# An attention and mixture-of-experts block: down product behind the first up product, mask products a step later, weight loads behind the high half

## The chip, the cores and the metric

The kernel runs on one core of a Trainium2 chip. The metric is the device time of one execution in microseconds. TensorE multiplies, VectorE and ScalarE do the elementwise work, GpSimd subtracts and issues gathers, SyncE's queue issues most transfers. The engines run their own instruction lists in order and meet at semaphores.

## The reference, cut to what matters

The block is an adaptive layer norm with linear attention, then a second layer norm with a feed-forward part of eight routed experts (two per token) and one shared expert:

```python
h = _layernorm(x) * (1 + ca) + sa
x = x + ga * attn(h)                      # linear attention, 16 heads of 32
h = _layernorm(x) * (1 + cb) + sb
scores = sigmoid(h @ gate_w.T)
idx = top_k(scores + router_bias, 2); w = scores[idx] / sum(scores[idx])
out = sum over the two experts of w * (silu(h @ W1[e]) * (h @ W3[e])) @ W2[e]
shared = (silu(h @ sw1.T) * (h @ sw3.T)) @ sw2.T
x = x + gb * (out + shared)
```

There are 4096 tokens of width 512; an expert has an inner width of 352, the shared expert of 704.

## The kernel before

All matrices are kept as a high and a low half in float16, and a product is three matmuls (high by high, high by low, low by high; lines 84 to 86). Tokens are worked in 32 tiles of 128.

The kernel has four stages. First the attention, a loop of slots `s`, in which tile s is projected and tile s - 8 is finished. From slot 32 on, only the finishing is left (the tail, slots 32 to 42), and the shared expert starts beside it. Then the shared expert goes on alone while the router picks experts and makes the token list. Then the routed experts run over 71 slot tiles. At the end the shared expert's last seven chunks run beside the combining of the results.

The shared expert works in chunks of two tiles, and a chunk in six steps, one for each 128 columns of the inner width (the sixth is 64 wide). Steps are numbered through: q = 6n + j. Each step has one piece on each engine:

- TensorE, `up(q)`: 24 products (12 in a sixth step) into one of three PSUM banks. It waits for `multiply(q - 3)`, which frees the bank.
- ScalarE, `activate(q)`: the silu from PSUM into `s_act`, of which there are two buffers; it waits for `up(q)` and for `low(q - 2)`. Then `high(q - 1)`, the cast of the previous step's product into the high half of `s_at`. With j = 0 it waits for the previous chunk's down product, since `s_at` has one buffer for each j.
- VectorE, `multiply(q)`, then `low(q - 1)`, the low half of `s_at`.
- Once per chunk TensorE's `down(n - 1)` multiplies the six pieces of `s_at` of the finished chunk by `sw2`: for each of its two tiles 17 products, in the order of j, each j of the first tile waiting for its low half. VectorE's `add(n - 1)` then joins it to the residual `s_xs`, and SyncE stores it and loads the next.

`down_due(q)` says at which steps down and add are issued: at j = 1 in the tail (q below 22), at j = 2 after it. Chunk 9's step 54 is left out; its down product runs among the experts.

Beside the steps run other things, in a table `beside` on VectorE: the selection of the experts (steps 22 to 24), the counts (`add_runs` and `place`, steps 25 and 26). In step 24 TensorE forms the ranks from `both`. From step 27 to step 42 VectorE makes the masks of two tiles in each step (`masks`: `lane_is` and two `tile_is` for each tile, lines 870 and 873; four buffers, freed by the products), between `multiply(q)` and `low(q - 1)`, and TensorE multiplies them in the same step (line 1381). In step 43 (`LIST_STEP`) `list_tokens` reads the sum and gives `slot_token`, on which the experts' gathers and the last 22 weight pieces wait (they lie where the names of the router lie).

The experts' weights, 88 pieces, are loaded into a ring of four staging buffers (`w_stage`) by loads issued on ScalarE's queue (`w_loads`, line 1056), each after the piece four before it has been converted. ScalarE casts each (line 1075). For pieces 22 to 65 it also rescales it in place (line 1078), and GpSimd subtracts (line 468); for the others VectorE makes the low half (line 688). `w_turn(q)` spreads the pieces over the steps: 44 over the steps up to `LIST_STEP`, the last 22 over the steps from there to step 50.

The orders of the engines in steps 22 to 53 are written out by hand:

Of the kernel before, what the change touches and what calls it, by code (L numbers as in the profile page):

```python
# [17 lines left out]
TILES = T // P  # L18
# [5 lines left out]
SH_TILES = 6  # L24
# [18 lines left out]
TAIL_STEPS = STEPS_PER_SLOT * TAIL  # L43
CHUNKS = TILES // 2
EARLY = 9
EARLY_STEPS = SH_TILES * EARLY
X_RING, QT_RING, HT_RING, XR_RING, X2_RING, H2T_RING, STAGE_RING, W_RING, Y_RING, YB = 4, 9, 3, 2, 3, 3, 6, 4, 4, 8
# [7 lines left out]
LISTED = 3  # L55
PICKED = 4
BIG = 1e30
LIST_STEP = TURNS_FROM + TILES // TURNS_PER_STEP
LAST_PIECES = 3
SHARED_PIECES = (E - 2) * WP  # L60
GB_LOADS = 16 * (4 + B)
# [57 lines left out]


def down_due(q):
    return q >= SH_TILES and q % SH_TILES == (1 if q < TAIL_STEPS else 2) and q // SH_TILES != EARLY


def list_turn(q):
    first = TURNS_PER_STEP * (q - TURNS_FROM)
    return range(first, first + TURNS_PER_STEP) if 0 <= first < TILES else range(0)
# [22 lines left out]
def sync_program(nc, m, sp):  # L150
# [196 lines left out]
    for q in range(EARLY_STEPS, SH_TILES * CHUNKS):  # L347
        n, j = q // SH_TILES, q % SH_TILES
        if j == 1:
            load_h(n + 1)  # L350
        if down_due(q):
            store_xs(n - 1)
            load_xs(n)
        r = early_turn(q)
        if r is not None:
            store_out(r)
            load_xc(r + Y_RING)
# [154 lines left out]
def vector_program(nc, m, v):  # L512
# [194 lines left out]
    for s in range(-3, TILES + TAIL):  # L707
# [34 lines left out]
        if s >= TILES:  # L742
            q = STEPS_PER_SLOT * (s - TILES)
            multiply(q)
            low(q - 1)
            if down_due(q):
                add(q // SH_TILES - 1)
        h2_low(t - 2)
        v_low(s)
# [26 lines left out]
        if s >= TILES:  # L776
            q = STEPS_PER_SLOT * (s - TILES)
            for p in w_turn(q):
                w_low(p)
            multiply(q + 1)  # L780
            low(q)
            if down_due(q + 1):
                add((q + 1) // SH_TILES - 1)
            for p in w_turn(q + 1):
                w_low(p)
# [110 lines left out]
    for q in range(TAIL_STEPS, EARLY_STEPS):  # L896
        multiply(q)
        for t in list_turn(q):
            masks(t)
        low(q - 1)  # L900
        if q > LIST_STEP:
            for p in w_turn(q):
                w_low(p)
        for work in beside.get(q, ()):
            work()
        if down_due(q):
            add(q // SH_TILES - 1)
    low(EARLY_STEPS - 1)

# [29 lines left out]
    for q in range(EARLY_STEPS, SH_TILES * CHUNKS):  # L939
        n, j = q // SH_TILES, q % SH_TILES  # L940
        multiply(q)
        if q > EARLY_STEPS:
            low(q - 1)
        if down_due(q):
            add(n - 1)
        t = early_turn(q)
        if t is not None:
            combine(t)
# [4 lines left out]
def scalar_program(nc, m, act):  # L953
# [88 lines left out]
    def high(q):  # L1042
        if q < 0:
            return
        n, j = q // SH_TILES, q % SH_TILES
        w = step_width(j)
        act.wait_ge(m.act_done, q + 1)
        if j == 0:
            at_least(act, m.sy_done, 2 * n)
        act.activation(m.s_at[0:w, j, 0, :], m.s_act[0:w, q % 2, :], ACT.Copy).then_inc(m.at_hi, 1)  # L1050
# [9 lines left out]
    def w_loads(last):  # L1060
        nonlocal w_next
        while w_next <= last:
            w_load(w_next)
            w_next += 1
# [24 lines left out]
    for s in range(-3, TILES + TAIL):  # L1089
# [48 lines left out]
                w_load(p)  # L1138
        if s >= TILES:
            q = STEPS_PER_SLOT * (s - TILES)  # L1140
            w_loads(q + W_RING - 1)
            activate(q)
            high(q - 1)
            h2_high(t - 2)
            convert_weights(q)
            w_loads(q + W_RING)
            activate(q + 1)
            high(q)
            convert_weights(q + 1)
# [8 lines left out]
    act.wait_ge(m.logits_ready, 1)  # L1158
    act.activation(m.scores[:, :, :], m.logits[:, :, 0:E], ACT.Sigmoid).then_inc(m.scores_ready, 1)
    for q in range(TAIL_STEPS, EARLY_STEPS):  # L1160
        if w_turn(q):
            w_loads(w_turn(q)[0] + W_RING - 1)
        activate(q)
        high(q - 1)
        convert_weights(q)
    high(EARLY_STEPS - 1)

# [34 lines left out]
def tensor_program(nc, m, pe):  # L1202
# [164 lines left out]

    for q in range(TAIL_STEPS, EARLY_STEPS):
        up(q)
        if q == TAIL_STEPS + 2:  # L1370
            pe.wait_ge(m.both_ready, 1)
            pe.wait_ge(m.r_consts, 5)
            for part, lhs in ((0, m.before), (1, m.ones)):
                nc.tensor.matmul(m.ps_r[:, part, :], lhs[:, :], m.both[:, :, :].rearrange("p t e -> p (t e)"),
                                 start=True, stop=True).then_inc(m.ranks_done, 1)
        if down_due(q):
            down(q // SH_TILES - 1)
        for t in list_turn(q):
            for k in range(TOP):
                pe.wait_ge(m.pair_ready, (1 + TOP) * t + 2 + k)  # L1380
                nc.tensor.matmul(m.ps_list.rearrange("p t n -> p (t n)"), m.lane_is[:, t % PAIR_RING, k, :],  # L1381
                                 m.tile_is[:, t % PAIR_RING, k, :, :].rearrange("p t n -> p (t n)"),
                                 start=t == 0 and k == 0, stop=t == TILES - 1 and k == TOP - 1, skip_group_check=True).then_inc(m.pair_used, 1)
# [343 lines left out]
```

## Time and profile before

| | us |
|---|---|
| median of three runs | 1451.88 |
| lowest and highest run | 1448.08, 1453.30 |
| profiled execution | 1449.57 |
| its span | 1447.8 |
| busy in the span: TensorE products | 1264.5 |
| VectorE | 666.1 |
| ScalarE | 435.1 |
| GpSimd | 438.4 |
| mean granted clock of TensorE | 0.942 |

Busy times are those of the profile; ends of matmuls are modelled, so TensorE's share is an upper value. The profile also divides the span into 40 slices of 36 us, and gives each wait the operation that ended it. A number behind a time in brackets is idle time of the engine ahead of the row.

In the time of the span the stages lie as follows: the tail of attention from 436 to about 577 us, the shared expert with router and token list from there to 828, the routed experts from 838 to 1268, the last stage from there to the end.

### The profile page before, as it was taken

Reading aid. Unit: us, or ns where it says so; the run is one execution under the profiler, and the core shown is the slowest. Engines: PE = TensorE matmul, PEld = TensorE weight load, DVE = VectorE, ACT = ScalarE, POOL = GpSimd, SP = SyncE. Lnnn points to the kernel's source line nnn. Section 1 sums busy time; section 2 is a strip of 40 time slices with the busy share of each in tenths; the row PEclk is TensorE's granted clock in tenths of the full one; section 3 lists DMA queues with packets and bytes.
Section 4 is the critical chain, followed back from the end, with each engine's and each line's share of the span. In section 5 each row is a group of like instructions: output and inputs, shape, how many; then the busy total and the mean of one; then the engine's idle time right before and its main releaser. Section 6 shows DMA issues by size and latency. Waiting matters only on the chain.

```text
span 1447.8 us, 25298 instructions
## 1 busy us (share of the span) xinstructions
PE 1264.5 (87%) x9054; PEld 795.8 (55%) x9054; DVE 666.1 (46%) x1338; ACT 435.1 (30%) x913; POOL 438.4 (30%) x411
## 2 busy tenths in 40 slices
PE   6898998998997789556658789999999999989998
PEld 2545655665665557333325446566656665566664
DVE  4555867777776646653444521111111111125455
ACT  2433434443433324422232412222222222211211
POOL 1213655655553322321121011111111111146542
PEclk9999999999998989867778889999999999999999
DMA  5714787888968557222121555655555556569886
GB/s 183 223 48 123 186 182 186 215 188 185 209 174 239 168 144 217 63 89 67 50 76 44 162 129 132 133 134 132 132 131 138 140 134 133 114 191 243 227 216 171
DMA packets 269205, 219.09 MB, mean 151 GB/s; under 512 B 188496, under 2 KB 200784, under 8 KB 268572
## 3 DMA queue, kind: packets, MB, share of 16 engines
q1 hardware_dynamic: 241560, 158.45, 42.9%
q0 software_dynamic: 12848, 35.40, 10.7%
q10 hardware_dynamic: 14680, 23.62, 5.4%
q8 instruction: 80, 1.31, 0.4%
q14 instruction: 37, 0.30, 0.1%
HBM read 116.69 MB, written 56.94 MB: 120 GB/s over the span
## 4 chain that ended last, share of the span: by engine, by line
PE 53%; DVE 12%; DMA 10%; POOL 10%; issue 9%; ACT 4%; SPq 1%; ACTq 0%; DVEq 0%; POOLq 0%
PE ps_o L84 6%; PE ps_o L85 6%; PE ps_o L86 6%; PE ps_vs L84 5%; PE ps_vs L86 5%; PE ps_vs L85 5%; DMA xt<-g 2%; DVE tile_is L873 2%; DMA yb<-y_d,slot 2%; DMA wp_raw<-in_wproj_t 2%; PE ps_kh L84 2%; PE ps_vh L84 2%; PE ps_vh L85 2%; PE ps_vh L86 2%; PE ps_kh L86 2%
## 5 line engine op out<-in xcount | busy, mean ns | idle before, releaser
L84 PE MATMUL ps_o<-w_all,xt 128*128 x568 | 178.7, 315 | 15.6 <-DMA xt<-g 15.2
L477 POOL DMA_INDIRECT g<-h_d,slot_token x71 | 67.9, 956 | 391.2 <-DMA xt<-g 348.7
L85 PE MATMUL ps_o<-w_all,xt 128*128 x568 | 178.7, 315 | 0.0
L86 PE MATMUL ps_o<-w_all,xt 128*128 x568 | 178.6, 314 | 0.0
L920 DVE TENSOR_TENSOR at<-ps_y,at 128x384 f16<-128x384 f32 x71 | 39.6, 558 | 176.6 <-ACT at L1176 176.6
L1181 ACT ACTIVATE y<-ps_vs,slot_weight 128x512 f32<-128x512 f32 x71 | 48.8, 688 | 230.6 <-PE ps_vs L86 230.6
L915 DVE SCALAR_TENSOR_TENSOR a<-ps_o,a 128x352 f32<-128x352 f32 x71 | 37.3, 525 | 173.3 <-PE ps_o L86 173.3
L468 POOL TENSOR_TENSOR w_all<-w_stage,w_all 128x352 f16<-128x352 f32 (+2 forms) x44 | 45.0, 1033 | 166.5 <-ACT w_stage L1078 166.1
L84 PE MATMUL ps_qh<-ht,wqkv 128*128 128x128 f16 x512 | 87.5, 219 | 7.3 <-DVE qt L555 4.9
L656 DVE TENSOR_TENSOR s_at<-s_act,s_at 128x256 f16<-128x256 f32 x80 | 35.3, 441 | 125.1 <-ACT s_at L1050 115.4
L84 PE MATMUL ps_kh<-s_ht,sh 128*128 128x256 f16 x256 | 78.1, 305 | 16.8 <-DVE s_act L644 9.6
L86 PE MATMUL ps_qh<-ht,wqkv 128*128 128x128 f16 x512 | 87.4, 219 | 0.0
L85 PE MATMUL ps_qh<-ht,wqkv 128*128 128x128 f16 x512 | 87.4, 219 | 0.0
L1381 PE MATMUL ps_o<-tile_is,lane_is 128*128 128x213 f16 x64 | 19.5, 307 | 73.2 <-DVE tile_is L873 72.0
L384 POOL TENSOR_TENSOR h<-cen,rows_f 128x512 f32<-128x512 f32 x32 | 40.6, 1270 | 134.6 <-ACT cen L958 121.5
L84 PE MATMUL ps_vs<-w_all,at 128*128 (+1 forms) x213 | 80.9, 380 | 0.0
L86 PE MATMUL ps_vs<-w_all,at 128*128 (+1 forms) x213 | 80.6, 378 | 0.0
L85 PE MATMUL ps_vs<-w_all,at 128*128 (+1 forms) x213 | 80.6, 378 | 0.0
L84 PEld LDWEIGHTS ps_o<-w_all,xt 128*128 128x128 f16 x568 | 55.8, 98 | 44.2 <-issue 17.9
L1050 ACT ACTIVATE s_at<-s_act 128x256 f16<-128x256 f32 x96 | 39.2, 408 | 130.2 <-PE ps_vs L1324 129.5
L85 PE MATMUL ps_kh<-s_ht,sh 128*128 128x256 f16 x256 | 77.9, 304 | 0.0
L86 PE MATMUL ps_kh<-s_ht,sh 128*128 128x256 f16 x256 | 77.7, 303 | 0.0
(242 smaller groups left out, 3402.6 us busy)
## 6 DMA issues: line engine op xcount, KB each, us to landing
y_d<-y SPq DMA_DIRECT2D x71, 256.0 KB, 3.3
w_stage<-in_w_d ACTq DMA_DIRECT2D x64, 176.0 KB, 2.4
xb<-in_x SPq DMA_DIRECT2D x32, 256.0 KB, 3.3
xr<-in_x SPq DMA_DIRECT2D x32, 256.0 KB, 4.1
x_d<-x SPq DMA_DIRECT2D x32, 256.0 KB, 3.4
h_d<-hl SPq DMA_DIRECT2D x32, 256.0 KB, 2.6
h2t_d<-h2t SPq DMA_DIRECT2D x32, 256.0 KB, 3.8
s_ht<-h2t_d SPq DMA_DIRECT2D x32, 256.0 KB
```

The costliest lines, as they stand in the source:

```text
L84: nc.tensor.matmul(out, lh, rh, start=first, stop=False, skip_group_check=True)
L85: nc.tensor.matmul(out, lh, rl, start=False, stop=False, skip_group_check=True)
L86: return nc.tensor.matmul(out, ll, rh, start=False, stop=last, skip_group_check=True)
L384: pool.tensor_tensor(m.h[:, i % 2, :], m.cen[:, i % 2, :], m.rows_f[:, (i // BT) % 2, SA, :], ALU.add).then_inc(m.h_done, 1)
L468: pool.tensor_tensor(dst[:, 1, :], m.w_stage[0:rows, p % W_RING, 0:cols], dst[:, 0, :], ALU.subtract).then_inc(m.w_lo, 1)
L477: pool.indirect_dma_start(m.g[:, t % 2, :], None, m.h2_d, bass.IndirectOffsetOnAxis(ap=m.slot_token[:, t:t + 1], axis=0)).then_inc(m.gathe ...
L656: v.tensor_tensor(m.s_at[:, j, 1, :], m.s_act[:, q % 2, :], m.s_at[:, j, 0, :], ALU.subtract).then_inc(m.at_lo, 1)
L873: v.scalar_tensor_tensor(out=m.tile_is[:, r, k, :, :], in0=m.tile_no[:, :, :], scalar=m.tile_of[:, k, t:t + 1], in1=m.values[:, k, t, :].u ...
L915: v.scalar_tensor_tensor(out=m.a[:, t % 2, 0:INTER], in0=m.ps_h3[:, 0:INTER], scalar=1.0 / SCALE, in1=m.a[:, t % 2, 0:INTER], op0=ALU.mult ...
L920: v.tensor_tensor(m.at[:, t % 2, 1, :, :], m.ps_a[:, :, :], m.at[:, t % 2, 0, :, :], ALU.subtract).then_inc(m.e_at_lo, 1)
L1050: act.activation(m.s_at[0:w, j, 0, :], m.s_act[0:w, q % 2, :], ACT.Copy).then_inc(m.at_hi, 1)
L1181: act.activation(m.y[:, t % 2, :], m.ps_ey[:, 0:C], ACT.Copy, scale=m.slot_weight[:, t:t + 1]).then_inc(m.ey_ready, 1)
```

## The change

The down product moves directly behind the first up product of the next chunk (j = 0) everywhere, the add of its result to j = 1. The products of the masks of step q - 1 are issued in step q; the rank products and `list_tokens` with `LIST_STEP` move one step later, which leaves six steps instead of seven for the last 22 weight pieces. On ScalarE the weight loads of a step are issued behind `activate(q)` and `high(q - 1)`; in the tail of attention the second call of `w_loads` in a slot is gone, and the next call makes up for it.

```diff
-LIST_STEP = TURNS_FROM + TILES // TURNS_PER_STEP
+LIST_STEP = TURNS_FROM + TILES // TURNS_PER_STEP + 1
...
 def down_due(q):
-    return q >= SH_TILES and q % SH_TILES == (1 if q < TAIL_STEPS else 2) and q // SH_TILES != EARLY
+    return q >= SH_TILES and q % SH_TILES == 0 and q // SH_TILES != EARLY
+
+
+def add_due(q):
+    return q >= SH_TILES and q % SH_TILES == 1 and q // SH_TILES != EARLY
...
# sync_program, and four places of vector_program with add(...)
-        if down_due(q):
+        if add_due(q):
             store_xs(n - 1)
             load_xs(n)
...
# scalar_program, tail
             q = STEPS_PER_SLOT * (s - TILES)
-            w_loads(q + W_RING - 1)
             activate(q)
             high(q - 1)
+            w_loads(q + W_RING - 1)
             h2_high(t - 2)
             convert_weights(q)
-            w_loads(q + W_RING)
             activate(q + 1)
             high(q)
             convert_weights(q + 1)
...
# scalar_program, steps 22 to 53
     for q in range(TAIL_STEPS, EARLY_STEPS):
+        activate(q)
+        high(q - 1)
         if w_turn(q):
             w_loads(w_turn(q)[0] + W_RING - 1)
-        activate(q)
-        high(q - 1)
         convert_weights(q)
...
# tensor_program
-        if q == TAIL_STEPS + 2:
+        if q == TAIL_STEPS + 3:
             pe.wait_ge(m.both_ready, 1)
...
         if down_due(q):
             down(q // SH_TILES - 1)
-        for t in list_turn(q):
+        for t in list_turn(q - 1):
```

## Rows read from the trace of the kernel before

**Rows 1.** Page, busy tenths and granted clock (tenths) in 40 slices of the span.

```profile
PE   6898998998997789556658789999999999989998
...
PEclk9999999999998989867778889999999999999999
```

**Rows 2.** Busy us by stretch: TensorE, loads, VectorE, ScalarE, GpSimd; then granted clock, DMA.

```profile
432.00:577.00 145.00, 122.46 (x929) 85.42 (x930) 85.45 (x180) 45.24 (x110) 41.85 (x38) 0.92 0.68 190
621.00:773.00 152.00, 91.95 (x456) 54.18 (x457) 67.03 (x134) 40.05 (x93) 30.82 (x30) 0.75 0.23 70
```

**Rows 3.** Waits 621 to 773: engine, line, releaser, total us, times, longest.

```profile
PE ps_o L1381 <- DVE tile_is L873: 72.0, 40, 13.3
...
ACT s_at L1050 <- PE ps_vs L1324: 28.1, 2, 14.9
```

**Rows 4.** Timeline, three mask steps and one add: start, length, engine, line, operation.

```profile
679.38 0.69 DVE L683 TENSOR_TENSOR s_xs<-s_t,s_xs 128x512 f32<-128x512 f32 x1
...
681.14 0.38 ACT L1036 ACTIVATE s_act<-ps_kh 128x256 f32<-128x256 f32 x1 [5.94 <-PE ps_kh L86]
...
681.56 0.42 DVE L644 SCALAR_TENSOR_TENSOR s_act<-ps_kh,s_act 128x256 f32<-128x256 f32 x1 [1.48 <-ACT s_act L1036]
...
685.16 0.41 DVE L656 TENSOR_TENSOR s_at<-s_act,s_at 128x256 f16<-128x256 f32 x1
...
768.37 0.39 ACT L1036 ACTIVATE s_act<-ps_kh 128x256 f32<-128x256 f32 x1 [7.17 <-PE ps_kh L86]
...
772.87 0.42 DVE L658 TENSOR_TENSOR s_at<-s_act,s_at 64x256 f16<-64x256 f32 x1
...
775.07 0.18 DVE L891 CAST eid<-eidf 1x71 int32<-1x71 f32 x1
```

**Rows 5.** Timeline of TensorE: two down products, and an up product.

```profile
659.68 0.38 PE L84 MATMUL ps_vs<-sh,s_at 128*128 128x512 f16 x1
...
718.43 0.27 PE L84 MATMUL ps_qh<-s_ht,sh 128*128 128x256 f16 x1
...
721.05 0.38 PE L84 MATMUL ps_vs<-sh,s_at 128*128 128x512 f16 x1
...
724.29 0.38 PE L1323 MATMUL ps_vs<-sh,s_at 128*128 128x512 f16 x1
...
728.48 0.39 PE L1324 MATMUL ps_vs<-sh,s_at 64*128 64x512 f16 x1
```

**Rows 6.** Timeline of VectorE: selection, counts, first masks.

```profile
589.06 0.42 DVE L821 TENSOR_TENSOR both<-choice 128x256 f16<-128x256 f32 x1
...
605.67 0.43 DVE L656 TENSOR_TENSOR s_at<-s_act,s_at 128x256 f16<-128x256 f32 x1 [9.87 <-ACT s_at L1050]
...
619.99 0.42 DVE L644 SCALAR_TENSOR_TENSOR s_act<-ps_kh,s_act 128x256 f32<-128x256 f32 x1
```

**Rows 7.** Durations min/median/max in ns: masks, subtractions; last, us from issue to landing.

```profile
L873 DVE SCALAR_TENSOR_TENSOR tile_is<-tile_no,tile_of,values x64: 425/438/2142, 620.7 to 771.5; 128x213 f16<-128x213 f16 x64
...
L468 POOL TENSOR_TENSOR w_all<-w_stage,w_all x32: 844/984/1308, 628.4 to 791.8; 128x352 f16<-128x352 f32 x23, 128x512 f16<-128x512 f32 x6, 96x512 f16<-96x512 f32 x3
...
DMA to landing us min/median/max: 2.1/2.4/5.9
```

**Rows 8.** Timeline, from the token list to the first expert product.

```profile
790.88 1.05 DVE L883 TENSOR_SCALAR slot_weight<-tokenf 128x71 f32<-128x71 f32 x1
...
827.04 0.69 DVE L688 SCALAR_TENSOR_TENSOR w_all<-w_stage,w_all 96x512 f16<-96x512 f32 x1 [0.20 <-ACT w_all L1075]
...
833.65 3.26 SPq L314 DMA_TRANSPOSE xt<-g  x2
...
838.25 0.47 PE L84 MATMUL ps_o<-w_all,xt 128*128 x1 [11.01 <-DMA xt<-g]
```

**Rows 9.** Waits 1300 to 1448.

```profile
PE ps_kh L84 <- DVE s_act L644: 6.1, 5, 1.2
```

**Rows 10.** Waits 447 to 577.

```profile
PE ps_o L84 <- issue: 15.3, 7, 4.4
```

More of the change, by code:

```diff
@@ L745, in vector_program @@
             low(q - 1)
-            if down_due(q):
+            if add_due(q):
                 add(q // SH_TILES - 1)
@@ L781, in vector_program @@
             low(q)
-            if down_due(q + 1):
+            if add_due(q + 1):
                 add((q + 1) // SH_TILES - 1)
@@ L905, in vector_program @@
             work()
-        if down_due(q):
+        if add_due(q):
             add(q // SH_TILES - 1)
@@ L943, in vector_program @@
             low(q - 1)
-        if down_due(q):
+        if add_due(q):
             add(n - 1)
```

## The prediction

> **What bounds the kernel now.** I read the page's slices first. TensorE is busy eight tenths or more in most slices, but only 5 to 6 tenths from the seventeenth to the twenty-first, and the granted clock falls with it [rows 1]. I then cut the span into stages [rows 2]. From 621 to 773 us TensorE is busy 92 of 152 us by modelled ends, VectorE 67, ScalarE 40 and GpSimd 31, at a granted clock of 0.75. No engine is full there; the engines take turns. The waits of this stretch name the turn [rows 3]: TensorE waited 72 us for the masks (`tile_is`), and ScalarE 28 us, in two waits, for a down product.
>
> The code gives the order behind these rows. At step q TensorE issues `up(q)`, a down product if one is due, then the mask products of that same step, and only then `up(q + 1)`. But the masks are made behind `multiply(q)`, which needs silu(q), which needs `up(q)`. So nothing of step q + 1 overlaps the masks. The second turn is the down product: it is issued behind `up(6n + 2)`, while `high(6n)` on ScalarE may not overwrite `s_at` before that product has read it. ScalarE stands until it ends, and with it the silu of the next steps and their masks.
>
> **The profiled execution.** It took 1449.57 us with a span of 1447.8; the median of the three runs is 1451.88, 2.3 above it. I work against 1449.57 and take the same number as the estimate for a median, since 2 us is inside the spread of the runs.
>
> **Part 1, the first masks.** The router's selection ends with `both` at 589.06 us. Then `low(24)` stands 9.87 us, until 605.67, for `down(3)`, and the multiply in front of the first masks starts at 619.99 [rows 6]. Changed, `down(3)` stands behind `up(24)`. Its last part needs `low(23)`, which VectorE reaches behind `both`, near 590.3. From there: 4.4 us for the 19 products behind that wait (724.29 to 728.7 in [rows 5]), 2.6 for `up(25)`, 0.8 to silu and multiply: `low(24)` near 598. The VectorE list from there to the first masks is 14.3 us long (605.67 to 619.99), so the masks start near 612: **8 us earlier**. The rank products, moved one step later, have `both` finished by then and cost TensorE nothing; what waits for them is `add_runs`, and they stand directly behind `up(25)`. `add` is now one step earlier and inside the same 14.3 us.
>
> **Part 2, the pace of a mask step.** With the products one step later, TensorE can do `up(q + 1)` while VectorE makes the masks of q. What is late next? ScalarE's `activate(q)` waits for `low(q - 2)`, the last instruction of VectorE's previous step (`s_act` has two buffers). So the cycle is silu, multiply, masks, low, and again silu, and its length stands in the rows: from silu at 681.14 to the end of the low at 685.57 is 4.4 us; the step that begins at 768.37 ends at 773.29, 4.9 us [rows 4]. In both the masks are stretched by GpSimd's subtractions beside them. I take 4.6. TensorE needs 2.6 for an up product at full clock (718.43 to 721.05) and about 0.4 for the mask products [rows 5], so it fits. ScalarE's own list in a step is four casts of 0.5 to 0.6, silu, high and two load issues, about 3.5 to 4 us, and now the two loads stand behind silu and high, so the wait for GpSimd's last subtraction (0.98 us each, [rows 7]) no longer delays silu.
>
> **Part 3, a mask step with a down product.** `down(n - 1)` needs `low(6n - 1)` after its first 15 products (3.2 us). On VectorE this low stands behind the two tiles' masks of step 6n. From silu(6n) to that low's end is again 4.4; then 4.4 for the 19 products, 0.5 for mask products, 2.6 for `up(6n + 1)` and 0.2 to its silu: 12.1 us. TensorE waits about 2 to 3 us inside the down product; that is the new wait this change brings. In return ScalarE no longer stands at `high(6n)`. The step behind it carries `add`, four instructions of 0.7 us [rows 4] and the gaps between them, 3.0 us. A period of six steps is 12.1 + 5 x 4.6 + 3.0 = 38.1 us. Before, the chain went through both turns, and the down products of two neighbouring chunks begin 61.4 us apart, at 659.68 and 721.05 [rows 5].
>
> **The sum to the list.** From the first multiply with masks: three steps of 4.6 (13.8), two periods (76.2), the down step 42 (12.1), then step 43 with multiply, low and name_tiles (2.4 from the low at 772.87 to the end of name_tiles at 775.25 [rows 4], and 0.3 for multiply) and add (3.0), 5.7, with the silu in front 6.0, and step 44 with `list_tokens`, 2.9: 111 us. Before, 619.99 to 791.9 (the last row of `list_tokens` [rows 8] and its end), 171.9. So **61 us** less, and the list is ready near 723 instead of 791.9.
>
> **Part 4, the last weights.** 22 pieces are converted behind the list, now in six steps instead of seven. Before, 791.9 to 827.7 [rows 8], 35.8 us, with 6 us of it standing for `down(7)`. Changed, `down(7)` stands behind `up(48)` and waits for VectorE; with four pieces in most steps and a ring of four, a step's loads land 2.4 us (2.1 to 5.9, [rows 7]) after their issue and little of that is covered. Bounds: 30 to 42; I take 35, a gain of **1**. From the last conversion to the first expert product is 10.5 us (827.7 to 838.25). The transposes start at 833.65 behind a store and a load of `s_xs` on SyncE's queue [rows 8]. `add(7)` comes one step earlier, so the store clears: **1**.
>
> **Part 5, the last stage.** There are five waits of 1.2 us of `up(6n + 6)` for `multiply(6n + 3)`, 6.1 in all [rows 9]. Behind a down product TensorE has 2.5 up products, 6.5 us, until it needs that multiply; VectorE works off `low(6n)`, combine and `add` first and is 7.7 us late. With `add` at step 6n + 1 VectorE begins the same list at the end of `up(6n + 1)`, and TensorE has 3.5 up products, 9.2 us: the five waits go, and the last down product, which meets VectorE still busy, gains about 1: **7**, at least 4. The low half that each moved down product needs ends about 1.6 us behind the up product, covered by its first 3.2 us. SyncE stores and reloads `s_xs` one step earlier with it; nothing in TensorE's waits of this stage comes from there.
>
> **Part 6, the tail of attention (432 to 577).** TensorE is full there at clock 0.92 [rows 2]; it loses 15.3 us in seven waits ahead of `attend` [rows 10], and slots with a down product at their end hide most of theirs. The change moves that cover three times from the slot's end to its middle: 1 us lost each; the loads behind the high half give some back. I take **+2**, bounds -3 and +6. My pace assumes full clock; if a fifth of the some 90 us of the mask stage runs at half clock and half of that reaches the chain, it costs a few us more: **+2**.
>
> Sum: 1449.57 - 8 - 61 - 1 - 1 - 7 + 2 + 2 = 1375.6; I forecast **1375 us**.
>
> **A rule against the pace.** In the trace a mask instruction takes 438 ns at the median and up to 2142 beside GpSimd; the stretch in a step is about 1.2 us [rows 4, 7]. The Trainium skill (SBUF — State Buffer, section "SBUF: two separate sides") says that VectorE with two inputs in SBUF and a reading GpSimd shut each other out for a whole instruction. Taken at its worst, both subtractions block the masks in full: that is rival 2.
>
> **The rivals.**
> 1. *Less stretch.* The subtractions slip to where VectorE waits anyway. A step without stretch is 3.4 instead of 4.6; half of this over 15 steps is 9 us, all of it 18: 1357 to 1366. Against it: casts and masks start from the same silu, as now. Chance 0.15.
> 2. *Full blocking, and a low clock.* Two subtractions of 0.98 in full are 2.0 instead of 1.2 us a step, 0.8 x 15 = 12; if the clock stays near 0.75, an up product of 4 to 5 us joins the cycle, some 8 more: 1387 to 1395. Chance 0.17.
> 3. *The last weights become the bound.* Six steps with exposed loads of 2.4 us and with add in between: 50 us instead of 35: 1390. Chance 0.06.
> 4. *The wait is only renamed.* VectorE's masks, not the order, set the stage, and products wait as before. Only parts 1 and 5 remain: 1435. VectorE at 67 of 152 us speaks against it. Chance 0.04.
> 5. *Slower.* The loads issued behind the high half land too late, since each is used one step later: then a step lasts the landing plus some 2 us. The mean step from 580 to 791 is 9.6 us, so this decides from landings of about 8 us on; at 10 each of 22 steps loses 2.4, less the 15 gained elsewhere: 1488. The longest landing is 5.9 [rows 7]. Chance 0.03.
>
> The forecast itself, 1366 to 1387, has 0.55. The range, 1353 to 1396, takes in rivals 1 to 3. Half a per cent (7 us) is about what a measurement of this kernel can tell from no change. Faster by more than that: all but 5 and a sliver of 4, 0.95; same 0.02; slower 0.03.
>
> **What would show it.** Right: the waits of the mask products for `tile_is` fall from 72 us to under 15; `high` no longer waits for a down product; down products in the mask stage contain a wait of 2 to 4 us for a low half; they lie near 38 us apart; the list ends near 723; the granted clock of the stage is near 0.9; the multiply waits of the last stage are gone. Wrong: a period above 45 us, a step above 5.5, or a last-weights stage above 42.

## The result, and the profile after

The changed kernel takes 1378.02 us (median; 1372.02 to 1379.86) against 1451.68 (1448.08 to 1453.3): a ratio of 0.949, with a 95% interval of 0.945 to 0.952. That is 74 us less; the forecast was 1375 us. Its profiled execution, the fastest of the four, took 1372.02 us with a span of 1370.3.

The page after, with the same lines as [rows 1]: busy tenths of TensorE and VectorE and the granted clock, in 40 slices.

```profile
PE   6998998998997889877787699999999999989998
...
DVE  4645777777776676676664211111111111126355
...
PEclk9999999999998999889898899999999999999999
```

The trough of 5 and 6 tenths from the seventeenth to the twenty-first slice is gone, 7 and 8 tenths stand in its place. The same stages as in [rows 2], by the columns TensorE, weight loads, VectorE, ScalarE, GpSimd, clock, DMA: the tail of attention, the mask stage, the last stage.

```profile
440.00:562.00 122.00, 111.26 (x887) 77.32 (x886) 79.61 (x161) 42.85 (x106) 40.69 (x34) 0.99 0.74 204
602.00:720.00 118.00, 94.06 (x574) 60.12 (x574) 78.44 (x154) 46.68 (x106) 33.39 (x33) 0.84 0.31 96
1225.00:1370.00 145.00, 134.86 (x990) 95.35 (x989) 75.10 (x145) 26.79 (x77) 71.29 (x54) 1.00 0.85 222
```

A table of stretches says more. I cut both traces at the same events: the first up product of step 0, that of step 22, the multiply of step 27 (the first masks), the end of `list_tokens`, the end of the last weight piece, the first expert product, the first up product of the last stage, and the end.

| stretch, us | before | after | difference | forecast |
|---|---|---|---|---|
| start to step 0 | 439.7 | 438.5 | -1.2 | 0 |
| tail of attention | 132.7 | 121.5 | -11.3 | +2 |
| selection, to the first masks | 47.6 | 41.6 | -6.0 | -8 |
| first masks to list | 171.9 | 118.1 | -53.8 | -61 and +2 |
| last weights | 35.8 | 35.6 | -0.2 | -1 |
| hand-over to the experts | 10.5 | 8.2 | -2.4 | -1 |
| experts | 430.5 | 431.3 | +0.8 | 0 |
| last stage | 179.1 | 175.6 | -3.4 | -7 |
| span | 1447.8 | 1370.3 | -77.5 | -74 |

In the mask stage the waits that answer to [rows 3] are these (602 to 706 us; engine, line, releaser, total, times, longest). Of the 20.6 us of the first line 7.9 belong to the very first masks. No wait of `high` for a down product is left; a wait inside the down products stands there instead.

```profile
PE ps_o L1384 <- DVE tile_is L877: 20.6, 14, 7.9
...
PE ps_vs L1326 <- DVE s_at L662: 9.3, 3, 3.8
```

A mask step in full, VectorE and then ScalarE, answering to [rows 4]:

```profile
644.37 0.42 DVE L648 SCALAR_TENSOR_TENSOR s_act<-ps_vh,s_act 128x256 f32<-128x256 f32 x1 [0.51 <-ACT s_act L1040]
...
645.04 0.78 DVE L877 SCALAR_TENSOR_TENSOR tile_is<-tile_no,tile_of,values 128x213 f16<-128x213 f16 x2
...
646.75 1.37 DVE L877 SCALAR_TENSOR_TENSOR tile_is<-tile_no,tile_of,values 128x213 f16<-128x213 f16 x2
648.05 0.41 DVE L660 TENSOR_TENSOR s_at<-s_act,s_at 128x256 f16<-128x256 f32 x1
```

```profile
643.95 0.38 ACT L1040 ACTIVATE s_act<-ps_vh 128x256 f32<-128x256 f32 x1 [2.02 <-PE ps_vh L86]
...
648.54 0.38 ACT L1043 ACTIVATE s_t<-ps_qh 64x256 f32<-64x256 f32 x1 [2.07 <-DVE s_at L660]
```

The step begins with silu at 643.95 and ends with the low at 648.46; the silu of the next one (line 1043, a sixth step) starts at 648.54. Each row of `tile_is` shows two of them: without GpSimd beside them the two take 0.78 us, and 1.37 or more with it. The gaps from one multiply to the next over steps 27 to 43, in us, are 3.3, 4.9, 4.6, **14.0**, 6.9, 4.9, 4.2, 5.0, 4.5, **15.2**, 6.9, 4.9, 5.0, 4.9, 4.5, **15.0**, 6.1; before they were 7.1, 6.6, 9.4, 9.7, 19.8, 9.0, 8.6, 7.6 and so on. The bold ones are the steps with a down product (down steps from here on); the ones behind them, 6.9 and 6.1, carry `add`.

One such down product on TensorE, answering to [rows 5]:

```profile
650.90 0.38 PE L84 MATMUL ps_vs<-sh,s_at 128*128 128x512 f16 x1
...
658.12 0.61 PE L1326 MATMUL ps_vs<-sh,s_at 128*128 128x512 f16 x1 [3.81 <-DVE s_at L662]
...
665.52 0.55 PE L1384 MATMUL ps_o<-tile_is,lane_is 128*128 128x213 f16 x4
```

It starts at 650.90, stands 3.81 us for the low that is behind the masks, and its last 19 products then take 7.4 us to the next instruction, where they took 4.4.

From the list to the last weight piece, answering to [rows 8]:

```profile
719.45 0.20 DVE L887 TENSOR_SCALAR slot_weight<-tokenf 128x71 f32<-128x71 f32 x1
...
752.89 2.32 DVE L692 SCALAR_TENSOR_TENSOR w_all<-w_stage,w_all 128x352 f16<-128x352 f32 x4
```

### The profile page after: what moved, and what is told of

It reads as the page before. It is cut to its first block, busy times and chain, and to the rows that moved or that the text cites. A ratio compares the mean times of both kernels' runs of the same rounds, so it can differ in the third digit from the quotient of the medians.

```text
span 1370.3 us, 25298 instructions
## 1 busy us (share of the span) xinstructions
PE 1240.9 (91%) x9054; PEld 785.3 (57%) x9054; DVE 667.8 (49%) x1338; ACT 436.2 (32%) x913; POOL 440.1 (32%) x411
## 4 chain that ended last, share of the span: by engine, by line
PE 54%; DVE 14%; DMA 10%; POOL 8%; issue 7%; ACT 3%; SPq 2%; ACTq 1%; DVEq 0%; POOLq 0%
PE ps_o L84 6%; PE ps_o L85 6%; PE ps_o L86 6%; PE ps_vs L84 5%; PE ps_vs L85 5%; PE ps_vs L86 5%; DMA xt<-g 3%; DVE tile_is L877 3%; DMA wp_raw<-in_wproj_t 2%; PE ps_vh L84 2%; PE ps_vh L86 2%; PE ps_vh L85 2%; DMA s_ht<-h2t_d 2%; PE ps_kh L84 2%; PE ps_kh L86 2%
## 5 line engine op out<-in xcount | busy, mean ns | idle before, releaser
L84 PE MATMUL ps_o<-w_all,xt 128*128 x568 | 178.3, 314 | 15.3 <-DMA xt<-g 15.2
L84 PE MATMUL ps_qh<-ht,wqkv 128*128 128x128 f16 x512 | 89.0, 221 | 6.5 <-DVE qt L559 3.6
L86 PE MATMUL ps_qh<-ht,wqkv 128*128 128x128 f16 x512 | 89.0, 221 | 0.0
L85 PE MATMUL ps_qh<-ht,wqkv 128*128 128x128 f16 x512 | 89.0, 221 | 0.0
L84 PE MATMUL ps_kh<-s_ht,sh 128*128 128x256 f16 x256 | 72.7, 284 | 12.7 <-DMA s_ht<-h2t_d 12.0
L84 PEld LDWEIGHTS ps_o<-w_all,xt 128*128 128x128 f16 x568 | 55.6, 98 | 44.0 <-issue 18.1
L648 DVE SCALAR_TENSOR_TENSOR s_act<-ps_vh,s_act 128x256 f32<-128x256 f32 x32 | 13.5, 422 | 121.3 <-ACT s_act L1040 121.3
L85 PE MATMUL ps_kh<-s_ht,sh 128*128 128x256 f16 x256 | 72.5, 283 | 0.0
L84 PE MATMUL ps_vs<-sh,s_at 128*128 128x512 f16 x160 | 65.7, 411 | 7.4 <-DVE s_at L660 7.4
L86 PE MATMUL ps_kh<-s_ht,sh 128*128 128x256 f16 x256 | 72.4, 283 | 0.0
L86 PEld LDWEIGHTS ps_o<-w_all,xt 128*128 128x128 f16 x568 | 55.8, 98 | 28.8
```

What stands on the lines that cost most here:

```text
L84: nc.tensor.matmul(out, lh, rh, start=first, stop=False, skip_group_check=True)
L85: nc.tensor.matmul(out, lh, rl, start=False, stop=False, skip_group_check=True)
L86: return nc.tensor.matmul(out, ll, rh, start=False, stop=last, skip_group_check=True)
L648: v.scalar_tensor_tensor(out=m.s_act[:, q % 2, :], in0=m.ps_h[j % 3][:, 1, :], scalar=1.0 / SCALE, in1=m.s_act[:, q % 2, :], op0=ALU.mult, ...
```

## The experiments

All of these are timed beside the kernel before on the same chip, and each has a profile cut in the same way. The chip is not the same for all of them (the kernel before had medians of 1449.1, 1454.3 and 1453.5 us beside them), so rows are compared by their ratios. `noloads` and `nodowns` are the whole change without one part; the runs below them in the table add something to the whole change.

| stretch, us | tail | selection | masks to list | weights | hand-over | last stage | median | ratio to before (95%) |
|---|---|---|---|---|---|---|---|---|
| before | 132.7 | 47.6 | 171.9 | 35.8 | 10.5 | 179.1 | | |
| whole change | 121.5 | 41.6 | 118.1 | 35.6 | 8.2 | 175.6 | 1378.0 | 0.949 (0.945 to 0.952) |
| products | 131.2 | 43.4 | 116.3 | 31.1 | 10.6 | 184.0 | 1387.2 | 0.956 (0.951 to 0.962) |
| downs | 138.6 | 45.3 | 158.7 | 37.8 | 7.9 | 179.3 | 1436.6 | 0.990 (0.987 to 0.993) |
| loads | 118.2 | 45.6 | 162.6 | 35.6 | 10.7 | 181.2 | 1432.3 | 0.988 (0.982 to 0.993) |
| noloads | 139.6 | 42.4 | 118.9 | 33.7 | 8.1 | 176.5 | 1390.8 | 0.959 (0.952 to 0.966) |
| nodowns | 118.7 | 44.2 | 108.8 | 32.3 | 11.1 | 181.4 | 1372.7 | 0.942 (0.940 to 0.945) |
| nopool | 121.0 | 34.9 | 90.2 | 35.6 | 8.0 | 182.8 | 1347.0 | 0.925 (0.922 to 0.927) |
| lowfirst | 122.1 | 41.9 | 98.5 | 34.9 | 8.0 | 176.3 | 1362.5 | 0.936 (0.934 to 0.939) |
| xclate | 121.0 | 41.4 | 117.9 | 35.3 | 8.0 | 171.0 | 1371.7 | 0.942 (0.940 to 0.944) |
| best | 120.2 | 41.4 | 101.4 | 34.9 | 8.2 | 170.0 | 1346.1 | 0.927 (0.924 to 0.930) |
| best2 | 119.5 | 44.6 | 108.3 | 32.3 | 10.7 | 179.2 | 1366.0 | 0.939 (0.936 to 0.942) |

The experts, whose code no edit touches, lie between 429.4 and 433.3 us in all of them. The last stage of `products` and `loads`, whose code there is that of before, is 184.0 and 181.2 against 179.1, and `nopool` has 182.8 where the whole change, with the same code there, has 175.6. So single profiles of that stage differ by up to 7 us. What varies is TensorE's waits for the next chunk's tokens (`s_ht`), 5.7 us in all in `before`, 10.0 in the whole change and 12.8 in `nopool`, and stretches at the lower clock. For the last stage single waits are read, and no small differences of its length. The profiles of `loads` and of the whole change are those of their fastest runs, 8.8 and 6.0 us below their medians, so their stretches come out short in sum by about as much.

### Each part alone

**The products one step later, alone:**

```diff
-LIST_STEP = TURNS_FROM + TILES // TURNS_PER_STEP
+LIST_STEP = TURNS_FROM + TILES // TURNS_PER_STEP + 1
...
-        if q == TAIL_STEPS + 2:
+        if q == TAIL_STEPS + 3:
...
-        for t in list_turn(q):
+        for t in list_turn(q - 1):
```

> Before with one part of the change alone: mask products, rank products and list_tokens one step later; down product, add and weight loads stay where they were. My theory (the cycle of a mask step is silu, multiply, masks, low on ScalarE and VectorE, 4.6 us, once TensorE need not wait for the masks of its own step): mask steps without a down product last 4.4 to 5, the waits of the mask products fall from 72 to under 25 us, while ScalarE still stands about 10 us per chunk at high for the down product; the stretch from the first masks to the list shrinks by 40 to 50 us of the 54 that the whole change gave, the total is near 1403. Rival (the down product's place is what holds the stage; moved products only rename the wait): period of a chunk stays above 55 us, total above 1430. The tail of attention is as before (132 us).

Measured: 1387.2 us. The list stretch falls by 55.6 us, to 116.3, as far as with the whole change (118.1); I had expected 40 to 50. Mask steps last 3.3 to 5.0 us. Its waits from 602 to 720 us are these:

```profile
PE ps_o L1381 <- DVE tile_is L873: 30.9, 23, 9.6
...
ACT s_at L1050 <- PE ps_vs L1324: 19.5, 2, 9.8
```

Of the first line 9.6 us are the first masks again. ScalarE still stands 9.8 us for a down product, twice in this window, and the down steps last 13.9, 13.9 and 14.5 us, no more than the 14.0 to 15.2 of the whole change. The rival, that the wait is only renamed, is out: the place of the products alone gives a ratio of 0.956, the whole change 0.949.

**The down product and add, alone** (`down_due` at j = 0, `add_due` at j = 1, as in the change):

> Before with the down product and add alone moved to the first and second step of a chunk. My theory: mask steps still take 8 to 9 us each, since the products wait for the masks of their own step; a chunk in the mask stage shortens by about 4 us (61.4 to 57), the first masks come 6 earlier, the last stage is 3 to 4 shorter; total near 1430. Rival (the place of the down product carries the gain): under 1410. On the tail of attention, which became 11 us shorter against my forecast: if the place of the down product did that, the tail is near 122 here; if the order of the weight loads did it, it is 132 or more here.

Measured: 1436.6 us. Mask steps stay at 7.5 to 9.8 us; the first two down steps fall from 19.8 and 18.1 to 12.4 (the third, with a wait of 1.8 us in its down product, to 14.5), and a chunk from 61.4 to 57.5, as expected. The total is some 6 us above the estimate. The first masks come 2.2 us earlier in the selection stretch instead of 6, the last stage gains nothing (its multiply waits are gone, but its waits for `s_ht` are 11.0 us instead of 5.7), and the tail lasts 138.6 us, 6 more than before.

```profile
PE ps_o L84 <- issue: 16.2, 7, 4.4
...
PE ps_vs L1327 <- DVE s_at L662: 2.7, 1, 2.7
```

Two rows of the tail (447 to 577 us): the idle time ahead of `attend` rises by 0.9 over [rows 10], and a wait of 2.7 us for the low half appears in the third down product. With a second wait of 0.5, where the kernel before had one of 0.7, and with its last 19 products behind them at a granted clock of 0.59, in 7.5 us instead of 4.6, this down product lasts 14.2 us instead of 8.7. That is nearly all of the 6 us.

**The weight loads behind the high half, alone** (the two edits of `scalar_program`):

> Before with the weight loads alone moved behind the high half. Theory A on the tail of attention: silu(q) and silu(q + 1) stood behind load issues that wait for VectorE's last weight half, and with them attend; then the tail is 8 to 11 us shorter here (near 122) and the idle time ahead of attend falls from 15 to under 10 us. Theory B: the down product's place did it; then the tail stays near 132. In the mask stage I expect 2 to 4 us. Total near 1438 by A, 1448 by B.

Measured: 1432.3 us; theory A holds, and by more than I gave it: the tail is 118.2 us, 14.5 less.

```profile
PE ps_o L84 <- issue: 6.9, 6, 1.5
```

The longest of these waits (447 to 562 us) was 4.4 us before and is 1.5 now. In the kernel before, silu itself waited for VectorE's weight half, 25.6 us in all from 447 to 577 us; neither of these two lines is left here:

```profile
ACT s_act L1036 <- DVE w_all L688: 15.0, 5, 4.5
ACT s_t L1039 <- DVE w_all L688: 10.6, 3, 3.8
```

This is what stood ahead of the longest wait of `attend` in the kernel before, on ScalarE:

```profile
501.55 0.33 ACTq L1056 DMA_DIRECT2D w_stage<-in_w_d  x1
501.99 0.38 ACT L1036 ACTIVATE s_act<-ps_kh 128x256 f32<-128x256 f32 x1 [4.54 <-DVE w_all L688]
...
503.09 0.17 ACT L1014 ACTIVATE logits<-ps_o 128x16 f32<-128x16 f32 x1
```

The load's wait for VectorE's weight half held silu, high, a weight cast and `logits_out`, and `attend`, at 503.37, needs the last of these. The waits were also long enough for the clock. From 445 to 555 us the granted clock is 1.00 here. It was 0.94 in the same window both of `before` and of `downs`, where two slots run in part at 1.2 GHz behind waits of 4.4 and 3.1 us. The rows of `loads` and then of `downs`:

```profile
445.00:555.00 110.00, 101.57 (x816) 70.44 (x817) 75.68 (x154) 40.63 (x101) 37.84 (x32) 1.00 0.78 214
```

```profile
445.00:555.00 110.00, 93.53 (x711) 64.30 (x710) 63.72 (x134) 33.90 (x84) 33.87 (x30) 0.94 0.65 179
```

The mask stage is shorter, too: 162.6 us against 171.9, where I had expected 2 to 4 us. How much of these 9.3 us is the edit's own was not separated; the profile is that of the fastest run.

### Each part left out

**Without the loads' move:**

> The changed kernel with the weight loads put back in front of silu and high. By theory A (the order of the loads shortened the tail): tail back to 130 to 133 us, mask steps longer by about 0.7 us since silu again stands behind GpSimd's last subtraction, in all 1390 to 1398. By theory B (the down product shortened it): tail near 122, total near 1383.

Measured: 1390.8 us, theory A again. The tail is 139.6, which is more than I expected: the moved down product, whose third one in the tail has waits of 0.5 and 2.7 us as in `downs`, comes on top of the 131.2 of `products`. The mask steps are no longer than with the whole change (118.9 against 118.1), so there I was wrong: in 602 to 745 us silu waits 5.3 us in all for GpSimd's subtractions and 34.4 for VectorE's lows, the later of the two in most steps.

**Without the down product's move:**

> The changed kernel with down product and add put back to their old steps: products and loads moved, nothing else. From the four parts so far (stretch of attention's tail 132.7 before, 131.2 with products alone, 138.6 with downs alone, 118.2 with loads alone; first masks to list 171.9, 116.3, 158.7, 162.6) theory: the three parts don't add; once the products are moved, the moved down product brings nothing in the mask stage and costs 3 to 6 us in the tail. Then this kernel's tail is 116 to 119, its list stretch 113 to 117, and its total is at or below that of the whole change: 1368 to 1376. Rival (my prediction: moved down products pay in the mask stage and the last stage): list stretch above 122, total above 1385.

Measured: 1372.7 us, 0.942 with an interval that ends where that of the whole change (0.945) begins. The tail is 118.7 and the list stretch 108.8, 9.3 us **shorter** than with the down product moved. Its waits from 600 to 750 us, which takes in the stretch of the last weights:

```profile
ACT s_at L1050 <- PE ps_vs L1323: 31.9, 4, 9.8
PE ps_o L1380 <- DVE tile_is L873: 30.6, 23, 11.3
```

Here ScalarE stands for four down products, 31.9 us in all, and yet the stage is faster. While ScalarE stands, TensorE runs the down product without a wait, at the full clock; the down steps last 12.9, 12.9 and 13.2 us, against 14.0 to 15.2. So in the mask stage the moved down product did not take a wait away. It put one on TensorE in exchange for one on ScalarE, and that on TensorE costs more. Of the 9.3 us, 5.3 lie in the three down steps and 1.5 in the two add steps behind them; about 1.5 is a third add, which comes ahead of the list in the whole change and behind it here.

Elsewhere it goes both ways: without the moved down product the tail is 2.8 and the last weights 3.3 us shorter, but the selection stretch is 2.6 us longer, the hand-over 2.9 and the last stage 5.8, the last of these within its spread. So over the whole kernel the two are close: the intervals just meet, and the profiled spans are 1371.3 and 1370.3 us.

### What sets a mask step

**GpSimd out of the way** (whole change; it leaves out the low halves of the 44 weight pieces that GpSimd treats):

```diff
-        pool.tensor_tensor(dst[:, 1, :], m.w_stage[0:rows, p % W_RING, 0:cols], dst[:, 0, :], ALU.subtract).then_inc(m.w_lo, 1)
+        pool.tensor_tensor(dst[:, 1, 0:1], m.w_stage[0:rows, p % W_RING, 0:1], dst[:, 0, 0:1], ALU.subtract).then_inc(m.w_lo, 1)
...
-            act.activation(staged, staged, ACT.Copy, scale=SCALE).then_inc(m.w_scaled, 1)
+            act.activation(dst[:, 1, :], staged, ACT.Copy, scale=0.0).then_inc(m.w_scaled, 1)
```

> The changed kernel, in which GpSimd subtracts only one column of each of the 44 weight pieces it treats, and ScalarE's rescale writes zeros into the low half instead (same length); the low halves of these weights are left out of the result. Theory (VectorE's masks are stretched 1.2 us a step by GpSimd's subtractions beside them): steps of 4.5 to 5.0 become 3.4 to 3.8, first masks to list shrinks from 118 to about 101, total near 1361. Rival (the step is set by ScalarE's list of casts and load issues, about 4 us): steps stay above 4.1, list stretch above 109.

Measured: 1347.0 us; steps of 3.3 to 3.7 us, as the theory said, and a list stretch of 90.2, 11 below the expected 101. The groups of the whole change and then of this kernel, 600 to 700 us (busy, mean ns):

```profile
L877 DVE SCALAR_TENSOR_TENSOR tile_is<-tile_no,tile_of,values 128x213 f16<-128x213 f16 x64 | 42.2, 700 | 0.0
L472 POOL TENSOR_TENSOR w_all<-w_stage,w_all 128x352 f16<-128x352 f32 x23 | 21.2, 926 | 54.2 <-ACT w_stage L1082 53.7
```

```profile
L877 DVE SCALAR_TENSOR_TENSOR tile_is<-tile_no,tile_of,values 128x213 f16<-128x213 f16 x61 | 23.9, 434 | 0.0
...
L472 POOL TENSOR_TENSOR w_all<-w_stage,w_all 128x1 f16<-128x1 f32 x30 | 10.4, 346 | 70.1 <-ACT w_all L1082 70.1
```

A `tile_is` takes 434 ns on average instead of 700, and none is longer than 440. ScalarE's list is the same in both, and a step of 3.3 us fits over it, so the rival is out. What I had not counted is the down step: 11.1 us instead of 14.0 to 15.2, because the low on which the down product waits is behind the stretched masks, too. Without the stretch its wait is 0.7 to 1.4 us instead of 1.7 to 3.8, and its last 19 products keep the full clock. The selection stretch is 6.7 us shorter as well, and the last stage 7 longer.

**The low in front of the masks** (whole change, VectorE, steps 22 to 53):

```diff
         multiply(q)
+        low(q - 1)
         for t in list_turn(q):
             masks(t)
-        low(q - 1)
```

> The changed kernel with VectorE's low(q - 1) in front of the masks of step q instead of behind them. Theory (the cycle goes through low: silu(q + 1) waits for low(q - 1), and each down product waits 3.8 us for a low that stands behind masks): the waits inside the down products of the mask stage go from 1.7, 3.8 and 3.8 to under 0.5, a down step from 14 to 15 us to about 11, the other steps from 4.7 to 4.3; list stretch from 118 to 103 to 107, total 1364 to 1368. Rival (VectorE is full in these steps, order inside it changes nothing but the down step): other steps stay at 4.7, list stretch 108 to 111. If VectorE now stands for high in each step, it is no shorter than 115.

Measured: 1362.5 us, the list stretch 98.5 us, below the 103 to 107 expected. The down products at 614.9, 649.2 and 683.2 us have no wait in them and take 7.8 us; their steps last 10.2 or 10.3 us, those with `add` 7.3 and 7.5, the others mostly 3.4 to 4.0 and 5.1. The waits that now lead are those of ScalarE for `up(6n + 1)`, which stands behind the down product, and with them VectorE's (600 to 706 us):

```profile
ACT s_act L1040 <- PE ps_vh L86: 31.7, 5, 7.9
...
DVE s_act L648 <- ACT s_act L1040: 20.0, 5, 6.0
```

This settles what the cycle ran through: it was the low, both for the next silu and for the down product.

### The last stage

**The loads of xc one combine later** (whole change, SyncE):

```diff
             store_out(r)
-            load_xc(r + Y_RING)
+            if r:
+                load_xc(r - 1 + Y_RING)
```

> The changed kernel with each load of xc in the last stage issued one combine later, so that SyncE's queue does not stand until the store just issued has landed. Theory (the 4.6 us of TensorE waits for s_ht that came in place of the multiply waits are the queue of SyncE: its load of the next chunk's tokens stands behind two such landings of 4 to 6 us): the s_ht waits after 1220 us go to under 1 us, last stage 175.6 to about 171, total 3 to 5 lower. Rival (the loads of s_ht themselves are slow beside the gathers): the waits stay.

In the whole change the five multiply waits of [rows 9] are gone, but this one has come (1225 to 1371 us):

```profile
PE ps_kh L84 <- DMA s_ht<-h2t_d: 4.6, 2, 3.0
```

SyncE's queue ahead of the first of the two:

```profile
1254.04 0.49 SPq L345 DMA_DIRECT2D out<-xc  x1
1258.55 0.32 SPq L341 DMA_DIRECT2D xc<-x2s_d  x1
1258.97 0.85 SPq L227 DMA_DIRECT2D s_ht<-h2t_d  x2
1259.87 0.90 SPq L239 DMA_DIRECT2D out<-s_xs  x2
```

The store of one result is issued at 1254.04 and lands at 1258.54. The load into the buffer that it frees waits for that and is issued at 1258.55. Only then come the next chunk's tokens (`s_ht`), whose chunk begins at 1266.03 instead of 1263.0. With the edit the wait is gone; the one left, 5.9 us, is that of chunk 10 at the stage's start, which both kernels before and after have, too (5.7 and 5.4). In this kernel, from 1190 us on:

```profile
PE ps_kh L84 <- DMA s_ht<-h2t_d: 5.9, 1, 5.9
```

Measured: 171.0 us for the stage and 1371.7 in all, a ratio of 0.942 against 0.949. The theory of the queue holds.

### A version that beats both

**best**: the whole change with low in front of the masks, xc loads one combine later, the down product back at j = 1 in attention's tail only, and chunk 10's tokens loaded before the experts:

```diff
-    return q >= SH_TILES and q % SH_TILES == 0 and q // SH_TILES != EARLY
+    return q >= SH_TILES and q % SH_TILES == (1 if q < TAIL_STEPS else 0) and q // SH_TILES != EARLY
...
     turn_g(1)
+    load_h(EARLY + 1)
     store_xs(EARLY - 1)
...
-        if j == 1:
+        if j == 1 and n > EARLY:
             load_h(n + 1)
```

> The changed kernel with what the runs pointed to: low(q - 1) in front of the masks, xc loads one combine later, the down product back at its old step in attention's tail only, and chunk 10's tokens loaded before the experts instead of behind SyncE's loads of the last stage. By the stretches of the runs so far: tail 118 to 119 (products and loads without downs gave 118.7), selection 42, list 98.5, weights 35, hand-over 8, experts 431.5, last stage 171 less the 5.9 us of its first wait for s_ht, 165: span near 1340, median 1338 to 1345. If the parts don't add, the list stretch is above 102 or the last stage above 169.

Measured: 1346.1 us, a ratio of 0.927, against 0.949 of the change. That is 1 us above the range. The last stage is 170.0 instead of 165, above the 169 named as the sign that the parts don't quite add: the wait for chunk 10's tokens is gone, but then the stage's first down product comes when VectorE is still behind with its lows, and two waits of 1.7 us and a stretch at 1.2 GHz take its place. The tail is 120.2 where 118 to 119 was expected, and the list stretch 101.4 against 98.5 in `lowfirst`, though the code there is the same: 3 us are the spread of that stretch between these two profiles.

Its page, with the same rows as for the change above: in the slices 18 to 23, where the change had 7 7 7 8 7 6 tenths, TensorE has 6 8 8 9 6 8.

```profile
PE   5998999998998899968896899999999999989998
...
DVE  3646767876876567677775211111111111126465
...
PEclk9999999999999899978898899999999999989999
```

**best2** has the down product and add at their old steps everywhere:

> The same four edits, but the down product at its old step everywhere. It asks what the moved down product is worth once nothing stands in its way. Theory (with low in front of the masks the moved down product no longer waits, so in the mask stage TensorE and ScalarE both go on): the other version's list stretch is 3 to 8 us shorter than here; here ScalarE stands at high for each down product, list 102 to 107, last stage 4 to 6 us longer by the multiply waits, total 1348 to 1356. Rival (as with products and loads alone, the down product's place is worth nothing): both within 4 us.

Measured: 1366.0 us, 10 above the expected range and 20 above `best`. The list stretch is 108.3 against 101.4, the last stage 179.2 against 170.0. So the moved down product, which cost 9 us in the mask stage behind the masks, gains 7 there once its low is in front of them. With it at its old place the low in front of the masks brings next to nothing (108.3 against 108.8 in `nodowns`).

## Why the prediction was right, and where it was not

The total is 3 us from the forecast. By its steps that is partly luck: two gains, in the mask stage and in the last stage, were forecast 11 us too large together, and the tail came out 13 us better than forecast, with the other sign.

- **What bounds the stage**: right. The mask products waited for masks of their own step, and `products` alone gives 0.956. The waits fell from 72 to 20.6 us, 12.7 without the first masks; the sign said under 15. The pace of a mask step was forecast at 4.6 and measured at 4.2 to 5.0. The list ends at 719.6 us, forecast near 723.
- **The period**: two down steps lie 40.7 and 41.2 us apart in the multiply gaps above, against 38.1 forecast and a bound of 45; by the starts of the down products it is 37.4 and 41.5. The granted clock of the stage is 0.84 against "near 0.9".
- **Part 1**: right in direction, 6.0 instead of 8, but only in part by the cause that it names. The down product behind the selection waits 3.3 and 2.8 us for lows, and then runs its last 19 products in 7.1 instead of 4.6 us. The later rank products, which it put at nothing, give more: `products` alone gains 4.2 us in this stretch, `downs` alone 2.2. In the kernel before TensorE stood 10.4 us for `both`; in `products` it is 5.5, and in the whole change there is no such wait:

```profile
PE ps_o L1374 <- DVE both L821: 10.4, 1, 10.4
```

- **Part 3**: the mechanism was right, one term mis-sized. A down step was to last 12.1 us and lasts 14.0 to 15.2, with a wait of 1.7, 3.8 and 3.8 us for the low. I had taken the 19 products behind it at the full clock; they take 6.2 to 7.4. The three down steps are 8 us longer than forecast in all, and that is the difference between 61 and 54; the other steps add up as forecast. The sentence "In return ScalarE no longer stands" weighed the two sides wrongly: `nodowns` shows that in this stage the exchange loses 9 us.
- **Clock**: I gave +2 us to up products at half clock (by the shares that the sentence names it would be about 4.5: a fifth of 90 us at half clock loses 9, and half of that reaches the chain). Four up products of steps 27 to 43 did run at half clock, and three of them took 4.5 to 5.0 us instead of 2.8. But each ended before the low for which silu waits as well, or within 0.1 us of it, so they cost next to nothing; it is the down products that pay.
- **Part 4**: the sum is right within 1 us. It is again made of two sides: with six steps and the down product at its old place the last weights take 31.1 and 32.3 us (`products`, `nodowns`), and the moved one, which waits 2.9 and 4.6 us for lows, brings them back to 35.6. In return the hand-over takes about 8 us in every kernel with the moved down product, and 10.5 to 11.1 in every one without.
- **Part 5**: the five multiply waits went, and one of the two in the last down product. The step that failed is "nothing in TensorE's waits of this stage comes from there": when a chunk shrank from 23.5 to 22.2 us, SyncE's queue brought the tokens of two of the five chunks behind it 3.0 and 1.6 us too late.
- **Part 6**: wrong in sign, by one of its two halves. The moved down product, 1 us three times, was about right: the whole change has a tail of 121.5 us, `nodowns` 118.7, and the down products at 508.84 and 542.82 each wait 0.9 us for a low. (Alone it costs 6 us, as shown under `downs`.) The failed step is the loads behind the high half, "give some back": -14.5 us alone, and 18.1 us lost when left out. The prediction counted the 15.3 us ahead of `attend` and did not say what they waited for; ScalarE's timeline at 501.55 shows the load that waits for VectorE. The row of the whole change (447 to 562 us), which answers to [rows 10]:

```profile
PE ps_o L84 <- issue: 8.6, 7, 1.5
```

  Seven waits as before, 8.6 us in all, and none longer than 1.5.
- **Rivals**: rival 1 (less stretch) did not occur, and its size was too small: the stretch is worth 28 us in this stage, not 18. Rival 2's longer stretch did not occur either; of its slow clock, the part inside the down products did. Rival 5, loads landing too late: the landings in the mask stage and the last weights had a median of 2.6 us and none above 4.9.

What stays open: how much of the 9.3 us that `loads` is shorter in the mask stage is the edit's, and why the last stage's waits for `s_ht` differ by several us between kernels with the same code there.

## What to carry to other kernels

When a product is moved ahead, look at what its last operand is queued behind on the engine that makes it; here one line moved on VectorE turned the moved down product from a loss of 9 us into a gain of 7 in the mask stage. A load issue whose buffer wait stands in front of an engine's critical work passes that wait on, here up to 4.5 us, though the issue itself takes only 0.3 us: put it behind. And the gains of the parts of a change can't simply be added: the same edit can pay or cost by what stands beside it, so each is worth a run alone and one left out.

## What the runs showed of the hardware

- The last 19 products of a down product (512 columns each) take 4.6 us to the end of the last at a granted clock of 1.00. They did so behind single waits of 0.7 to 1.5 us inside that down product (`nopool`, `downs`, the tails). Behind single waits of 1.7 and 1.8 us they took 6.3 us (whole change, `xclate`, `downs`), behind 3.8 and 3.9 us 7.1 to 7.5 us (whole change, `noloads`), partly at 1.2 GHz, at a mean granted clock of 0.59 to 0.73. Two waits of 1.17 us in the last down product were followed by either: 4.6 us in `before`, 5.5 to 5.8 in `products`, `loads` and `nodowns`. So the wait alone does not tell.
- VectorE's `tile_is` took 434 ns in `nopool`, and none took over 440. Beside GpSimd's subtractions of 926 ns it took 700 ns on average and up to 2140. In the whole change 25 of the 64 are longer than 1 us, and every one of them ends 0.23 or 0.24 us behind the end of a subtraction. That agrees with the Trainium skill (SBUF — State Buffer, section "SBUF: two separate sides"), by which one of the two is shut out for a whole instruction.
- A load issue that waits holds everything behind it on its queue: in the last stage of the whole change, at a DMA share of 0.85, a store issued at 1254.04 landed 4.5 us later, and the load that needed its buffer and two unrelated loads of `s_ht` were issued only then.
